# Attention's value product in 32-column tiles, and one copy, turn and normalise for sixteen heads

## The reference

```python
def windowed_attention(q, k, v, window_size):          # bh = 8*16, S = 256, D = 8, window 64
    for i in range(0, S, w2):                          # w2 = 32, w4 = 16
        start = max(0, i - w4)
        end = min(S, i + window_size - w4)
        attn = jax.nn.softmax(jnp.einsum('bqd,bkd->bqk', qw * scale, kw), axis=-1)
        wo = jnp.einsum('bqk,bkd->bqd', attn, vw)
        # neighbouring windows overlap by half: the overlap is blended with a linear ramp
        ...
ctx = windowed_attention(q, k, v, WIN)
out = ctx @ wproj + bproj + residual
```

## Time and profile before

| what | value |
|---|---|
| time, median of three runs | 371.27 us (369.61 to 377.07) |
| span of the profiled execution, first to last instruction | 361.3 us |
| mean granted clock of TensorE over the span | 0.887 |
| busy: TensorE, VectorE, ScalarE | 305.9, 244.1, 152.3 us |
| from gather_context of step 7 to the end | 125.6 us |

### The profile page before, as it was taken

How to read it: one execution, slowest core, us unless ns; L and a number is a source line. 1 busy time by engine, 2 the same in 40 slices (tenths; PEclk the granted TensorE clock), 3 DMA queues, 4 the chain that set the end, 5 groups by cost and what they waited for, 6 DMA issues and landing times.

```text
span 361.3 us, 10050 instructions
## 1 busy us (share of the span) xinstructions
PE 305.9 (85%) x3668; PEld 231.7 (64%) x3668; DVE 244.1 (68%) x709; ACT 152.3 (42%) x298; POOL 78.6 (22%) x115
## 2 busy tenths in 40 slices
PE   2256697999898998997898979888787989989993
PEld 1123554777676876876657757556576878868892
DVE  2454605837849759488456584858887899698986
ACT  2135073337346174463551635465455313824220
POOL 4443101302304104032020011030553012202020
PEclk9766588569789699799886999999999999999998
DMA  6009386270360903505308100000000000100000
GB/s 188 24 2 201 95 175 164 79 127 4 105 98 2 185 12 98 100 6 144 60 3 181 23 5 2 2 2 2 0 2 0 2 1 0 31 0 23 8 29 29
DMA packets 38540, 20.01 MB, mean 55 GB/s; under 512 B 5604, under 2 KB 38120, under 8 KB 38504
## 3 DMA queue, kind: packets, MB, share of 16 engines
q1 hardware_dynamic: 38504, 19.53, 24.7%
HBM read 11.13 MB, written 8.13 MB: 53 GB/s over the span
## 4 chain that ended last, share of the span: by engine, by line
PE 47%; DVE 22%; issue 9%; SPq 9%; DMA 7%; ACT 4%; POOL 1%; DVEq 0%; ACTq 0%; POOLq 0%
PE bank L637 5%; PE bank L422 5%; PE bank L386 5%; PE bank L432 4%; PE bank L403 4%; DVE xh L1007 3%; PE bank L398 3%; SPq L293 3%; SPq L320 3%; DMA kst<-stack_scratch 3%; PE bank L442 3%; PE bank L619 3%; DVE acc L1342 3%; PE bank L620 2%; PE bank L621 2%
## 5 line engine op out<-in xcount | busy, mean ns | idle before, releaser
L1048 DVE TENSOR_REDUCE nm<-bank 128x8 f32<-128x512 f32 x64 | 43.3, 690 | 29.0 <-PE bank L386 28.3
L857 POOL TENSOR_TENSOR rs<-ve,mhalf 128x2 f32<-128x2 f32 (+1 forms) x24 | 19.8, 827 | 141.5 <-DVE ve L1004 134.7
L720 ACT ACTIVATE prob<-bank 128x512 f32<-128x512 f32 x64 | 37.8, 601 | 11.8 <-PE bank L403 10.0
L422 PE MATMUL bank<-prob,vb 128*64 128x128 f32 x512 | 40.7, 305 | 2.1 <-issue 1.6
L386 PE MATMUL bank<-kst,qst 48*64 48x64 bf16 x1024 | 31.0, 208 | 7.7 <-DMA kst<-stack_scratch 4.3
L809 ACT ACTIVATE sg<-bank 128x512 f32<-128x512 f32 x32 | 18.9, 600 | 43.6 <-PE bank L621 42.1
L637 PEld LDWEIGHTS bank<-wds,hh 128*128 128x128 f32 x256 | 32.3, 191 | 7.1 <-issue 5.5
L726 ACT ACTIVATE pvs<-bank 128x512 f32<-128x512 f32 x32 | 19.1, 596 | 41.9 <-PE bank L422 41.9
L386 PEld LDWEIGHTS bank<-kst,qst 48*64 48x64 bf16 x1024 | 24.4, 120 | 18.4 <-issue 18.0
L637 PE MATMUL bank<-wds,hh 128*128 128x128 f32 x256 | 33.7, 277 | 2.8 <-DVE acc L1342 2.3
L422 PEld LDWEIGHTS bank<-prob,vb 128*64 128x64 f32 x512 | 31.7, 151 | 4.4 <-issue 2.7
(11 more groups left out here) (139 smaller groups left out, 514.0 us busy)
## 6 DMA issues: line engine op xcount, KB each, us to landing
stack_scratch<-parts SPq DMA_DIRECT2D x16, 216.0 KB, 2.3
qst<-stack_scratch SPq DMA_DIRECT2D x16, 216.0 KB, 3.9
kst<-stack_scratch SPq DMA_DIRECT2D x16, 216.0 KB, 5.3
stack_scratch<-parts SPq DMA_DIRECT2D x16, 144.0 KB, 2.3
stack_scratch<-parts SPq DMA_DIRECT2D x16, 72.0 KB, 2.0
mrow<-mt SPq DMA_DIRECT2D x64, 4.0 KB, 1.7
out_x<-fin SPq DMA_DIRECT2D x4, 256.0 KB, 2.3
xs<-in_x SPq DMA_DIRECT2D x1, 896.0 KB, 6.7
```

Source lines behind the costliest of these rows:

```text
L422: m = pe.matmul(psv[WIN * (h2 % 2):WIN * (h2 % 2) + WIN, P * (h2 // 2):P * (h2 // 2) + P], vb[n][:, eo, H2 * par + h2, :, :, :], prob[gp % ...
L720: act.activation(prob[g // 2 % 2][:, :, g % 2, :], psb[g % 2][:].rearrange("p (h q) -> p h q", h=H2), ACT.Exp).then_inc(exp_done, 1)
L1048: dve.tensor_reduce(nm[:, g, :], psa[g % 2][:].rearrange("p (h k) -> p h k", h=H2), AX_X, ALU.max, negate=True).then_inc(max_done, 1)
```

## The change

Four things change together.

1. `probs_v` issues sixteen matmuls per gp where it issued eight: each takes one sel only, 32 stationary columns and 64 moving ones, and writes 32 partitions of psv. Four neighbours go to the four groups of 32 columns. Both par of one eo share the bank psv, so that one bank holds sixteen heads.
2. `copy_pv`, `turn_sums` and `normalise` are called twice a step, by eo, in place of four times by gp. A copy and four transposes are as large as before; the reciprocal and the factors are too. ctxn is written by one operation over 128 partitions and 256 elements in place of two over 64 partitions and 128 elements.
3. TensorE's and VectorE's orders: `turn_sums(b, 0)` stands behind a(3), `turn_sums(b, 1)` behind a(7) and right before `gather_context`. `normalise(b, 0)` stands behind maxima(3) and before `ln_b`, `cut_qk` and `copy_mt`; `normalise(b, 1)` behind maxima(7).
4. The counts on the semaphores, the blend factors' layout and the buffers' shapes follow.

```diff
             def probs_v(b, n, gp):
...
-                pe.wait_ge(pvs_ready, after(pvs_ready, 4 * b + gp))
                 eo, par = gp // 2, gp % 2
-                for h2 in range(H2):
-                    m = pe.matmul(psv[WIN * (h2 % 2):WIN * (h2 % 2) + WIN, P * (h2 // 2):P * (h2 // 2) + P],
-                                  vb[n][:, eo, H2 * par + h2, :, :, :], prob[gp % 2][:, h2, :, :],
-                                  start=True, stop=True)
+                if par == 0:
+                    pe.wait_ge(pvs_ready, after(pvs_ready, 2 * b + eo))
+                for hg in range(2):
+                    for sel in range(2):
+                        for ct in range(4):
+                            h2, at = 4 * hg + ct, S * par + P * hg + WIN * sel
+                            m = pe.matmul(psv[32 * ct:32 * ct + 32, at:at + WIN],
+                                          vb[n][:, eo, H2 * par + h2, sel, :, :], prob[par][:, h2, sel, :],
+                                          start=True, stop=True)
                 m.then_inc(pv_done, 1)
 
-            def turn_sums(b, gp):
-
-                pe.wait_ge(pvs_ready, after(pvs_ready, 4 * b + gp + 1))
-                pe.wait_ge(norm_step, after(norm_step, 4 * (4 * b + gp)))
-                for k in range(H2 // 2):
+            def turn_sums(b, eo):
+
+                pe.wait_ge(pvs_ready, after(pvs_ready, 2 * b + eo + 1))
+                pe.wait_ge(norm_step, after(norm_step, 3 * (2 * b + eo)))
+                for k in range(4):
                     m = pe.transpose(pst[:, k * P:(k + 1) * P], pvs[:, k, :], idf[:])
                 m.then_inc(pt_done, 1)
...
-            def copy_pv(b, gp):
-                act.wait_ge(pv_done, after(pv_done, 4 * b + gp + 1))
-                act.wait_ge(pt_done, after(pt_done, 4 * b + gp))
+            def copy_pv(b, eo):
+                act.wait_ge(pv_done, after(pv_done, 4 * b + 2 * eo + 2))
+                act.wait_ge(pt_done, after(pt_done, 2 * b + eo))
                 act.activation(pvs[:], psv[:].rearrange("p (k q) -> p k q", q=P), ACT.Copy).then_inc(pvs_ready, 1)
...
-                for sel in range(2):
-                    p = slice(WIN * sel, WIN * sel + WIN)
-                    dst = ctxn[p, eo, :, WIN * par:WIN * par + WIN].rearrange("p f (h d) -> p f h d", d=HD)
-                    src = sums[p, :, 2 * sel:2 * sel + 2, 0:HD].rearrange("p h f d -> p f h d")
-                    f = fac[p, :, 2 * sel:2 * sel + 2].rearrange("p h (f o) -> p f h o", o=1)
-                    dve.tensor_tensor(dst, src, f.broadcast_to([WIN, 2, H2, HD]), ALU.mult
-                                      ).then_inc(norm_step, 1)
+                dst = ctxn[:, eo, :, :].rearrange("p f (h d) -> p h f d", d=HD)
+                f = fac[:].rearrange("p h (f o) -> p h f o", o=1)
+                dve.tensor_tensor(dst, sums[:, :, :, 0:HD], f.broadcast_to([P, NH, 2, HD]), ALU.mult
+                                  ).then_inc(norm_step, 1)
```

More of the change, by code:

```diff
@@ L435, in gather_context @@
             def gather_context(b):
-                pe.wait_ge(norm_step, after(norm_step, 16 * (b + 1)))
+                pe.wait_ge(norm_step, after(norm_step, 6 * (b + 1)))
                 for eo in range(2):
@@ L473, in first @@
                 elif c == 2:
-                    pe.wait_ge(norm_step, after(norm_step, 16 * B))
+                    pe.wait_ge(norm_step, after(norm_step, 6 * B))
                 pe.matmul(bk[2 + c][:], w1s[:, c, :], h2t[:, GW * g:GW * (g + 1)], start=True, stop=True
@@ L530, in step @@
                 a(0)
-                turn_sums(b, 0)
                 a(1)
@@ L543, in step @@
                 a(3)
+                turn_sums(b, 0)
                 scores_b(b, n, 4)
                 scores_b(b, n, 5)
-                turn_sums(b, 1)
                 a(4)
@@ L580, in step @@
                 a(7)
+                turn_sums(b, 1)
                 gather_context(b)
@@ L1054, in copy_mt, with normalise @@
                 dve.tensor_copy(mt[:], (psa[0] if hf else w1b)[0:64, 0:64].bitcast(BF16)).then_inc(mt_ready, 1)
[L1056 to L1060, removed]
-                sums = pst[:].rearrange("p (h w v) -> p h w v", h=H2, v=VC)
+            def normalise(b, eo):
+                dve.wait_ge(pt_done, after(pt_done, 2 * b + eo + 1))
+                base = 6 * b + 3 * eo
+                sums = pst[:].rearrange("p (h f v) -> p h f v", h=NH, v=VC)
                 dve.wait_ge(norm_step, after(norm_step, base))
@@ L1168, in step @@
                 maxima_next(1)
-                normalise(b, 0)
                 if norm:
@@ L1173, in step @@
                 maxima_next(3)
+                normalise(b, 0)
                 if group is not None:
@@ L1183, in step @@
                     cut_qk(b + 2, 1)
-                normalise(b, 1)
                 if group is not None:
@@ L1192, in step @@
                 maxima_next(5)
-                normalise(b, 2)
                 maxima_next(6)
-                normalise(b, 3)
                 maxima_next(7)
+                normalise(b, 1)
                 if norm:
@@ L1414 @@
     ramp = np.linspace(0.0, 1.0, WIN // 2, dtype=np.float32)
-    alpha = np.ones((2, WIN, 2, 2, 2), np.float32)
+    alpha = np.ones((2, WIN, 2, 2), np.float32)
     vmask = np.ones((P, 2, 2), np.float32)
@@ L1421 @@
                 if w > 0:
-                    alpha[:, :WIN // 2, eo, sel, half] = ramp
+                    alpha[sel, :WIN // 2, eo, half] = ramp
                 if w < S // (WIN // 2) - 1:
-                    alpha[:, WIN // 2:, eo, sel, half] = 1 - ramp
+                    alpha[sel, WIN // 2:, eo, half] = 1 - ramp
     vmask[:PAD, 0, 0] = 0
```

20 lines of the change are left out of this document (8 added, 12 removed).

## The result

The changed kernel takes 392.6 us (median of 4 executions, 390.9 to 395.9), the kernel before 374.2 beside it (4 executions, 369.6 to 378.6). The ratio is 1.058 with an interval of 1.048 to 1.067: slower by 5.8%, where 364.4 us and a range up to 371.5 were forecast. Medians here are over all executions of a kernel; ratios leave out those that lie more than 1.5% above the fastest of the same kernel.

A forecast was written before the change was run, and what follows sets the result against it. Bound by TensorE, partly at half clock, and a loop through memory of 22.0 us. Step 0 -1.6, steps 1 to 5 -4.1, step 6 +0.4, step 7 -1.6: span 361.3 to 354.4, plus 10.0 gives 364.4 us; range 357.5 to 371.5.

The forecast's parts named there:

- (1): Probabilities times values on TensorE: a block takes 0.5 us, saving 0.4 at full clock and 0.9 at half.
- Rival (d): Four tiles run no faster than two in the value blocks: 367.5 us, chance 7%.
- (2): Fewer copies, turns, normalises: 9.5 us less of ScalarE; per step 1.2 less of TensorE and 2.7 less of VectorE.
- (3): Loop of q and k through memory to the next step's scores_a: 22.0 us at full clock, 24.2 when slow; not shortened.
- (4): Late last turn before gather_context: TensorE waits 1.4 to 1.5 us every step, covered by the loop in steps 1 to 5.
- two fast and three slow: Steps 1 to 5: two at 22.0 us, three at 24.2, together 116.6 us, or -4.1.
- step 7: Gate, one normalise, a turn and the last's difference leave the chain; first normalise delays the statistics by 0.5: -1.6 us.
- Rival (c): Slower: TensorE's thinner work holds the low clock for half its work in steps 1 to 5: 377.8 us, chance 9%.
- Rival (a): The clock stays high: steps 1 to 5 take 110.0 us, the kernel 357.8; chance 24%.
- (b): Wait for the stacks and slow clock feed each other in every one of steps 1 to 5: 368.8 us, chance 20%.
- The 10.0 us outside the span: Median of three runs, 371.27 us, lies 10.0 above the profiled span; added to the forecast span of 354.4.
- Code loading: Named as a way to be wrong: missing cover in code loading might show with 512 more matmuls and weight loads.

The follow-up runs named there:

- the order put back: Changed kernel with the last turn_sums moved back ahead of project_v and a(7), and the last normalise ahead of maxima(7): 384.4 us, before 374.1.
- The two late-turn runs: Kernel before with the last turn_sums moved right before gather_context, last normalise behind maxima(7): 428.0 us; the same plus three constant float32 matmuls in the wait: 384.8 us.
- filled: Changed kernel plus three constant float32 matmuls in its wait before gather_context: 383.6 us, before 375.8, ratio 1.015.
- the quartered blocks: Kernel before with each 64x128 value matmul cut into four of 32 stationary and 64 moving columns: 391.0 us, before 374.1.
- the four kernels with only the blocks changed: Kernel before with value blocks halved to the useful products (387.8 us), or matmuls cut into four 32x64 (391.0), two 64x64 (389.2) or two 32x128 (385.2).
- The filled kernel: Kernel before with the last turn_sums right before gather_context and three constant float32 128x128 matmuls between them: 384.8 us, before 375.8.
- narrow filler: Kernel before with the last turn_sums right before gather_context and one matmul of 384 moving through 32 stationary columns between them: 387.1 us, before 373.1.

## Why the prediction was wrong

**(1) The value block: right.** 0.65 us from first start to last end, forecast 0.65 to 0.8. The 32 records start (0.65 - 0.22)/31 = 0.014 us apart, with 0.22 the shortest record. Rival (d), tiles no faster than two, is out. So is the floor of about 25 ns between starts that the prediction quoted from the Trainium skill, TensorE: Matmul & The Clock Gate, section "Wait — 56ns, not 53.3ns?": by it a block would take an estimated 0.8 us.

**(2) Copy, turn, normalise: right in size.** The last operation takes 0.424 us (0.43 forecast), from the start of the reciprocal to ctxn's end it is 1.05 (132.89 to 133.94 in the chain, 1.05 forecast). ScalarE's sixteen copies less came to 9.5 us in them; its busy time fell by 7.7.

**(3) The loop through memory: not what bound.** I had a wait for the stacks in most of steps 1 to 5 and a step of 22.0 or 24.2. In steps 1 to 5 of the changed kernel there is none at all: its only wait for kst is in the preparation (2.5 us). The one other wait over 0.6 us in these steps, beside that before gather_context and the gap at the loop's turn, is a later scores_a's, in step 5, for VectorE's maxima:

```profile
208.36 0.64 PE L386 MATMUL bank<-kst,qst 48*64 48x64 bf16 x16 [1.13 <-DVE nm L1048]
```

TensorE's own work at half clock is longer than the loop. With the order put back the waits do come (2.0 us at 79.2, 1.85 at 136.6), so the loop was read rightly, for a kernel with a faster clock.

**(4) The end of the step: sized nearly right, priced wrong.** This is the step that failed, and with it the clock in the sum that rests on it. The wait is 1.22 us, 1.4 to 1.5 forecast, and it is there in all eight steps. I charged it as idle time alone, and hid it in steps 1 to 5 behind the loop. But it stands in what was an unbroken run of project_v, a(7) and gather_context in which the clock came back before. The two late-turn runs show what it can do: +52 us for a wait of 1.4, and 43 of them given back by filling it. I had seen that the low level followed waits, and took "two fast and three slow" steps from a mechanism seen once, in steps 4 and 5; the rows on how the clock rises again were in the same trace and I did not ask them. In the changed kernel the wait's share is 8 to 9 us (order put back, or filled); the rest of the slow clock in the sum has other causes, see below.

**The sum.** Step 0: -1.8 against -1.6. Steps 1 to 5: 140.4 against 116.6. Step 6: +5.2 against +0.4, step 7: +6.2 against -1.6; both were forecast at full clock and stand at 0.50 and 0.55. The clock is low for (1 - 0.56)/0.5 = 88% of step 1. So the term that was wrong is the clock: two fast and three slow steps and full clock behind them were forecast, and half clock for 88 to 90% of steps 1 to 5 and for 90 to 100% of 6 and 7 was measured. Rival (c) had such a clock, held low by thinner work and not by a wait, and gave 377.8 at half the work; its 9% was far too little, and its place, steps 1 to 5 alone, too narrow. That thinner work is the cause is not borne out: the quartered blocks do all of the old products and lose more. Rival (a), a clock that stays high, is out; of (b), the low clock with a wait for the stacks in every step, only the clock came. The 10.0 us outside the span was also ill founded: in all executions since it is 1.7 to 2.3, and the rest of the 10.0 is that the traced execution was one of the quickest. Added to the span it made up for that by luck; but the rows, and with them the share of slow steps, still came from a trace whose clock stood at 0.89, where 0.84 to 0.85 is usual.

**Code loading** was named as a way to be wrong, without a price. It has one: 4.49 us of idling at the loop's turn. With the order put back, writing the loop out gives 10 us; in the changed kernel itself it gives none. What that gap costs thus hangs on the clock too.

**What stays open.** The order explains 8 us of the changed kernel's 18, and with the loop's code 18. But these two do not add up one by one (the loop alone: 0), and the four kernels with only the blocks changed lose 13 to 17 us in the old order, with a gap of only 4 to 5 us at the loop. None of the four was run with its loop written out, which would tell how much of their loss hangs on the loop's code. That the blocks' form or length does this is not borne out: quartered blocks are as long as the old ones and lose most. More instructions are common to all four; whether and how these lower the clock (0.76 to 0.82 in the profiled executions), also in the steps behind the loop, was not isolated. Nor was why the changed kernel's clock rises at project_qk and falls 3.4 us later with no wait over 0.6 us in between.

## What to carry to other kernels

Before pricing a new wait on TensorE at its own length, look up in the trace where the granted clock rises, and what ran without a break just ahead of it: a wait put there can cost many times itself. If a wait has to stand there, work on constants in it may be cheaper than idling, even on a quarter of the array; elsewhere such work gained nothing. And compare the clock of a trace with those of the other executions before building on its rows: one trace can be of a rare one. Last, count the instructions that a loop's body gains: a body that no longer stays loaded shows as an idle piece with the releaser "issue" where the loop turns, and as more packets on the instruction queue.

## What the runs showed of the hardware

- TensorE stayed at half clock for 191 us while 96% busy, with one wait of 1.3 to 1.4 us a step (late turn). A busy share does not tell that the clock is high. The Trainium skill, TensorE: Matmul & The Clock Gate, section "HAM oscillation — how this bites in real kernels", ascribes a low clock to waits between bursts of matmuls, and its example waits for DMAs. The filled kernel agrees that a wait is the cause here (0.50 to 0.83 in step 2), though it is for VectorE; that so short a one in so busy a step is enough was new to me.
- Waits before gather_context of 0.56 to 0.72 us (narrow filler) and one of 1.61 us before a turn (step 7 of the kernel before) came at full clock, and it did not fall.
- A float32 matmul of 32 stationary columns runs beside three others. Records of 128 moving columns start 0.126 us apart over the full width (eight of 0.275 in 1.16 us) and 0.026 apart with 32 stationary columns (32 of them in 1.08 us). With 64 moving columns there are 32 in 0.65 us, and 64 in 1.10.
- The loop's body stayed loaded for TensorE at about 372 matmul records a step and seems not to have at 428, with issue gaps of 4.3 to 4.5 us; at 365 to 380 records no run has that gap.
